# Projection of a four-layer kernel: in every tile the eight input runs first and the eight gate runs after them, with the statistics of the tile's own batches among its gates, and a second skip buffer

## The chip, the cores and the metric

One NeuronCore of a Trainium2 chip runs the whole program. The metric is the device time of one execution in microseconds (us); lower is better. Three runs of the kernel before gave 4415.28, 4422.65 and 4423.95 us, with the median at 4422.65 us.

## What is computed

Four layers are applied with a residual sum each: a gated state-space layer (0), two attention layers (1 and 2), and again a gated state-space layer (3). There are 32 batches of 128 tokens, 512 wide. The change touches only the first phase, the projection, of layers 0 and 3. Of the reference it computes this:

```python
xr, gate = jnp.split(x @ W_in.T, 2, axis=-1)          # 512 -> 2 x 1024
xr = xr + t_emb[:, None, :]
xc = conv(xr, W_conv, 4 taps, causal, per channel) + b_conv
xc = jax.nn.silu(xc)
mu, var = xc.mean(-1), xc.var(-1)
xn = (xc - mu) / jnp.sqrt(var + 1e-05) * ln_g + ln_b
Bm, Cm, dt = jnp.split(xn @ W_xproj.T, 3, axis=-1)    # 1024 -> 48
y = scan(...) + D * xn
return y * jax.nn.silu(gate) @ W_out.T
```

The projection phase leaves in memory the normalised `xn` (as a high and a low part), the skip term `D * xn`, and `silu(gate)`; it keeps the 48 projected columns and the mean and variance of every token on the chip. The recurrence phase reads them.

## The kernel before

The phase works on tiles of four batches (512 tokens), eight tiles T = 0 to 7, with a queue written out by hand for each engine; semaphores are the only order between engines.

PE (TensorE). `project_x(T, it)` multiplies 128 of the 1024 input channels by the tile: an input run of 12 matmuls (three partial products over four slices) into one of the two banks `pxr`. `project_gate(T, c)` is a gate run, also of 12 matmuls: one batch, 512 of the gate channels. `turn(n)` transposes the convolved batch n into the one two-bank buffer `ptr` (8 transposes); it waits on `z`, until DVE has read batch n-1 out of it. `xproj` multiplies the tile by the 48-column weight, `xproj_turn` transposes its result. Layer 3 reads its input in rows, so `turn_x(T + 1, b)` transposes the next tile's input, batch by batch (4 transposes each), through the one bank `pp`; its wait on `low` is the count of batches that DVE has read out of that bank. Layer 0 gets its input already transposed and has no `turn_x`.

DVE (VectorE). `evacuate(T, it)` adds the embedding and empties the `pxr` bank; `add_taps` adds three convolution taps on `pacc`; `split_low` takes the low part of the next tile's input (in layer 3 out of the bank `pp`); `centre(n)` is the statistics of batch n out of `ptr`, ending with the subtraction of the mean into `xn` (signal `z`), for which the `xn` buffer of batch n-2 must be free on POOL and ACT. ACT (ScalarE) does the first tap, the silu of convolution and gates, the high part of inputs (`split_high`), `rescale` by the standard deviation and `halves` (high part of `xn` and its squares). POOL (GpSimd) does for each batch in order: `shift` (adds ln_b), `skip_term` (D times xn, into `dx`), the next batch's `factor` (the inverse root) and `low_half`. SP stores the batch: `store_batch` waits for both halves, issues four stores of `xo`, waits for the skip term and stores `dx`.

There is one `dx` buffer, so `skip_term(n)` waits until the store of the skip term of batch n-1 has landed. In tile 0 the eight input runs come first and then the gates; in tiles 1 to 6 input and gate runs alternate, with the statistics of the tile before between them; in tile 7 the input runs come first, with statistics of tile 6 between, then the gates with those of tile 7.

## Time and profile before

| | us |
|---|---|
| profiled execution, its own time | 4415.49 |
| its span | 4413.70 |
| median of three runs | 4422.65 |
| layer 0, projection, from its first matmul to the start of the next phase | 11.15 to 581.75 |
| layer 3, the same | 3025.78 to 3601.52 |
| tile 1 to tile 7, starts of the first run, layer 0 | 76.53 to 434.33 |
| the same, layer 3 | 3097.89 to 3452.88 |

The page puts PE at 88% busy over the span, DVE at 67%, POOL at 41% and ACT at 30%. The other phases are the same instructions in both kernels. The two projections take about 1147 us of the 4414, so what happens elsewhere can be left out, and times below are those within one projection.

### The profile page before, as it was taken

How to read it: one execution, taken by the hardware profiler on the slowest of the kernel's cores; microseconds unless marked ns; L12 is line 12 of the kernel's file. 1: busy time of each engine (PE TensorE's matmuls, PEld its weight loads, DVE VectorE, ACT ScalarE, POOL GpSimd, SP SyncE). 2: the span in 40 equal slices, each digit the busy share in tenths (PEclk: the TensorE clock that was granted, in tenths of full speed). 3: DMA queues.
4: the chain of work that ended last, by engine and by line, in shares of the span. 5: the costliest groups of instructions: out<-in, count | busy, mean ns of one | idle time of the engine just before them, and what ended most of it. 6: DMA issues, size and time to landing. Idle time of an engine off the chain costs nothing. (4 is left out here: it accounts for less than half of the span.)

```text
span 4413.7 us, 67605 instructions
## 1 busy us (share of the span) xinstructions
PE 3882.5 (88%) x23976; PEld 2362.8 (54%) x23976; DVE 2944.5 (67%) x3022; ACT 1316.5 (30%) x1951; POOL 1811.0 (41%) x1456
## 2 busy tenths in 40 slices
PE   8999639999997599999849999997999818999999
PEld 6776413343332477777626777775777512443334
DVE  4666458999994555655445566653566537999996
ACT  3554301111113233333233333332455411111111
POOL 2555435555552123332312333323345534555555
PEclk9999859999998799999979999998999967999999
DMA  3565545666652122221221222213466545556653
GB/s 112 222 237 221 205 144 182 187 188 188 180 181 94 52 64 74 73 72 61 71 90 46 73 73 72 70 51 126 153 245 220 208 168 171 184 186 190 187 180 114
DMA packets 270306, 619.81 MB, mean 140 GB/s; under 512 B 34144, under 2 KB 36704, under 8 KB 270080
## 3 DMA queue, kind: packets, MB, share of 16 engines
q1 hardware_dynamic: 270080, 616.75, 42.3%
q8 instruction: 148, 2.42, 0.2%
q14 instruction: 78, 0.64, 0.0%
HBM read 380.46 MB, written 236.19 MB: 140 GB/s over the span
## 5 line engine op out<-in xcount | busy, mean ns | idle before, releaser
L1123 DVE CUSTOM_DVE_ANT_0 l3r_g<-l3r_g,l3r_pv,l3r_cf 128x1024 f32<-128x1024 f32 x512 | 674.3, 1339 | 77.9 <-PE l3r_pv L985 52.6
L1123 DVE CUSTOM_DVE_ANT_0 l0r_g<-l0r_g,l0r_pv,l0r_cf 128x1024 f32<-128x1024 f32 x512 | 674.1, 1339 | 74.8 <-PE l0r_pv L985 50.3
L985 PE MATMUL l3r_pv<-l3r_x,l3r_wv 32*128 32x512 f32 x1024 | 261.7, 510 | 26.0 <-POOL l3r_wv L910 19.9
L997 PE MATMUL l3r_py<-l3r_g,l3r_cd 128*32 128x512 f32 x2048 | 282.5, 625 | 2.1 <-POOL l3r_cd L923 2.1
L985 PE MATMUL l0r_pv<-l0r_x,l0r_wv 32*128 32x512 f32 x1024 | 260.9, 509 | 25.6 <-POOL l0r_wv L910 20.2
L997 PE MATMUL l0r_py<-l0r_g,l0r_cd 128*32 128x512 f32 x2048 | 281.2, 622 | 1.6 <-POOL l0r_cd L923 1.6
L985 PEld LDWEIGHTS l3r_pv<-l3r_x,l3r_wv 32*128 32x128 f32 x1024 | 97.2, 187 | 328.2 <-issue 227.1
L985 PEld LDWEIGHTS l0r_pv<-l0r_x,l0r_wv 32*128 32x128 f32 x1024 | 97.1, 187 | 326.2 <-issue 223.6
L1723 DVE RECIPROCAL l1h_rec<-l1h_ps_o 128x256 f32<-128x256 f32 x64 | 112.3, 1754 | 120.0 <-PE l1h_ps_o L1526 119.9
L1723 DVE RECIPROCAL l2h_rec<-l2h_ps_o 128x256 f32<-128x256 f32 x64 | 112.3, 1754 | 120.0 <-PE l2h_ps_o L1526 119.8
L558 DVE SCALAR_TENSOR_TENSOR l3a_pacc<-l3a_pad,l3a_wconv,l3a_pacc 128x512 f32<-128x512 f32 x192 | 144.8, 754 | 35.8 <-ACT l3a_pacc L433 31.2
L558 DVE SCALAR_TENSOR_TENSOR l0a_pacc<-l0a_pad,l0a_wconv,l0a_pacc 128x512 f32<-128x512 f32 x192 | 144.8, 754 | 34.5 <-ACT l0a_pacc L433 29.9
L670 POOL TENSOR_TENSOR l3a_dx<-l3a_xn,l3a_drow 128x1024 f32<-128x1024 f32 x32 | 76.3, 2384 | 215.2 <-DMA dx_s<-l3a_dx 215.1
L101 PE MATMUL l1h_ps_p<-l1h_xh,l1c_wh 128*128 128x512 f32 x384 | 161.3, 420 | 3.4 <-DVE l1h_xl L1715 2.9
L101 PE MATMUL l2h_ps_p<-l2h_xh,l2c_wh 128*128 128x512 f32 x384 | 160.9, 419 | 3.4 <-DVE l2h_xl L1715 2.9
L670 POOL TENSOR_TENSOR l0a_dx<-l0a_xn,l0a_drow 128x1024 f32<-128x1024 f32 x32 | 76.3, 2384 | 211.2 <-DMA dx_s<-l0a_dx 211.2
L103 PE MATMUL l2h_ps_p<-l2h_xl,l2c_wh 128*128 128x512 f32 x384 | 152.3, 397 | 0.0
L103 PE MATMUL l1h_ps_p<-l1h_xl,l1c_wh 128*128 128x512 f32 x384 | 152.0, 396 | 0.0
L102 PE MATMUL l2h_ps_p<-l2h_xh,l2c_wl 128*128 128x512 f32 x384 | 151.4, 394 | 0.0
L102 PE MATMUL l1h_ps_p<-l1h_xh,l1c_wl 128*128 128x512 f32 x384 | 150.9, 393 | 0.0
L1781 POOL TENSOR_TENSOR l1h_st<-l1h_veps,l1h_mhalf 128x1 f32<-128x1 f32 x32 | 17.6, 551 | 323.2 <-DVE l1h_veps L1689 323.2
L1781 POOL TENSOR_TENSOR l2h_st<-l2h_veps,l2h_mhalf 128x1 f32<-128x1 f32 x32 | 17.6, 551 | 322.9 <-DVE l2h_veps L1689 322.9
(404 smaller groups left out, 9862.7 us busy)
## 6 DMA issues: line engine op xcount, KB each, us to landing
xhl_s<-l0a_xo SPq DMA_DIRECT2D x128, 512.0 KB, 4.6
l0r_x<-xhl_s SPq DMA_DIRECT2D x128, 512.0 KB, 12.0
xhl_s<-l3a_xo SPq DMA_DIRECT2D x128, 512.0 KB, 4.6
l3r_x<-xhl_s SPq DMA_DIRECT2D x128, 512.0 KB, 11.8
gate_s<-l0a_gate SPq DMA_DIRECT2D x64, 256.0 KB, 3.3
dx_s<-l0a_dx SPq DMA_DIRECT2D x32, 512.0 KB, 5.0
l0r_crow<-feed_s SPq DMA_DIRECT2D x64, 256.0 KB
l0r_dx<-dx_s SPq DMA_DIRECT2D x32, 512.0 KB, 13.7
```

The source lines that it names most:

```text
L101: pe.matmul(out, wh, xh, start=first, stop=False)
L102: pe.matmul(out, wl, xh, start=False, stop=False)
L103: return pe.matmul(out, wh, xl, start=False, stop=last)
L558: dve.scalar_tensor_tensor(out=a, in0=pad[:, it % 2, :, c:c + S], scalar=wconv[:, it, c:c + 1], in1=a, op0=ALU.mult, op1=ALU.add).then_inc ...
L670: pool.tensor_tensor(dx[:, :], xn[:, r, :], drow[:, :], ALU.mult).then_inc(dxm, 1)
L985: last = pe.matmul(pv[j % 2][:, h * HALF:(h + 1) * HALF], wv[r, q, 2 * t + j % 2, :], x[r, q, t, j % 2, :], start=True, stop=True)
L997: last = pe.matmul(py[j * JW:(j + 1) * JW, h * HALF:(h + 1) * HALF], cd[:, q, t, j, :], g[:, t, j, h * HALF:(h + 1) * HALF], start=t == 0, ...
L1123: dve._custom_dve(bass.dve_ops.TENSOR_ADD_SAT, out=g[:, t, j, :], in0=g[:, (t - 1) % TS, j, :], in1=pv[j % 2][:, :], s0=cf[:, q, t, 0, j:j ...
L1723: dve.reciprocal(rec[:, :], ps_o[:, 2 * S:4 * S]).then_inc(rec_ok, 1)
L1781: pool.tensor_tensor(st[:, r, 2:3], veps[:, r:r + 1], mhalf[:, :], ALU.pow).then_inc(rs_ok, 1)
```

## The change

In every tile the eight input runs come first and the eight gate runs after them. The statistics of the tile's own four batches (`turn`, `xproj`, `xproj_turn`, `centre`) stand among these gates, and no longer among the runs of the following tile. The gates alternate between the banks `pg` and `pxr[1]` in all tiles (before: in the first and last). DVE evacuates run it+1 before it adds the taps of run it, in all tiles. The next tile's input is transposed after the input runs 4 to 7 (layer 3). The dt weight is folded after run 2 of tile 0, before: after run 4. The skip term gets a second buffer, the `stage` buffer that held weights, so that it waits for the store of batch n-2. In SP's queue the load of tile T + 1 stands at the start of tile T, behind the stores of the first two batches of tile T - 1 and ahead of those of its last two (the load of tile 1: among the weights of tile 0).

```diff
+        xo_st, dx_st = ph.sems("xo_st", 2), ph.sems("dx_st", 2)
         block = ph.block()
...
+        skip = (dx[:, :], stage[:, :, :].rearrange("p a n -> p (a n)"))
...
                 sp.wait_ge(dxm, n + 1)
-                sp.dma_start(dx_v[n // GB, n % GB, :, :, :], dx[:, :]).then_inc(dx_st, 16)
+                sp.dma_start(dx_v[n // GB, n % GB, :, :, :], skip[r]).then_inc(dx_st[r], 16)
...
-                    if it == 0:
-                        load(T + 1)
-                    store_gate(T, it)
-                    if it % 2 == 0 and TB * (T - 1) + it // 2 >= 2:
-                        store_batch(TB * (T - 1) + it // 2 - 2)
...
+                if c == 6:
+                    load(1)
+            for T in range(NT):
+                if 0 < T < NT - 1:
+                    load(T + 1)
+                if T:
+                    store_batch(TB * T - 2)
+                    store_batch(TB * T - 1)
+                for c in range(KI):
+                    store_gate(T, c)
+                    if c == 5:
+                        store_batch(TB * T)
+                    if c == 7:
+                        store_batch(TB * T + 1)
             store_batch(B - 2)
             store_batch(B - 1)
             for r in range(2):
                 sp.wait_ge(g_st[r], 16 * NT * KI // 2)
                 sp.wait_ge(xo_st[r], 64 * B // 2)
-            sp.wait_ge(dx_st, 16 * B)
+                sp.wait_ge(dx_st[r], 16 * B // 2)
...
-                if n == KI + 1:
-                    pe.wait_ge(g_ev, KI)
+                if it == 1:
+                    at_least(pe, g_ev, KI * T)
...
-                if in_a_row(T):
-                    at_least(pe, g_ev, n - 1)
-                    pe.wait_ge(xr_ev, KI * (T + 1))
-                else:
-                    at_least(pe, g_ev, n)
+                at_least(pe, g_ev, n - 1)
+                pe.wait_ge(xr_ev, KI * (T + 1))
...
                 pe.wait_ge(scaled, 3)
+                if rows:
+                    pe.wait_ge(low, 2 * TB)
...
                 if T:
                     pe.wait_ge(low, TB * T + b)
-                    pe.wait_ge(kept, 3)
                     at_least(pe, proj_ev, T - 1)
+                    if T == 1:
+                        pe.wait_ge(copied, 1)
...
-            for T in range(1, NT - 1):
+            for T in range(NT):
                 for it in range(KI):
                     project_x(T, it)
-                    if rows and it == KI - 1:
-                        turn_x(T + 1, TB - 1)
-                    project_gate(T, it)
-                    if it % 2 == 0:
-                        turn(TB * (T - 1) + it // 2)
-                    if it == 1:
-                        xproj(T - 1)
-                    if it == 3:
-                        xproj_turn(T - 1)
-                    if rows and TB <= it < KI - 1:
+                    if T == 0 and it == 2:
+                        fold_dt()
+                    if rows and it >= TB and T + 1 < NT:
                         turn_x(T + 1, it - TB)
...
+                for c in range(KI):
+                    project_gate(T, c)
+                    if T == 0 and c == 0:
+                        sum_weights()
+                    if c % 2 == 1:
+                        turn(TB * T + c // 2)
+                    if c == 2:
+                        xproj(T)
+                    if c == 4:
+                        xproj_turn(T)
...
+            for T in range(NT):
+                n = TB * T
                 for it in range(KI):
                     first_tap(T, it)
-                    if it == KI - 1:
-                        split_high(T + 1, TB - 1)
...
                     if it:
                         silu_conv(T, it - 1)
-                    elif T > 1:
-                        silu_conv(T - 1, KI - 1)
-                    n = TB * (T - 1) + it // 2
-                    silu_gate(T, it)
-                    if it == 2:
-                        copy_raw(T - 1)
-                    if TB <= it < KI - 1:
+                    if T:
+                        if it == 0:
+                            halves(n - 2)
+                        if it == 1:
+                            rescale(n - 1)
+                        if it == 2:
+                            halves(n - 1)
+                    if rows and it >= TB and T + 1 < NT:
                         split_high(T + 1, it - TB)
...
+                for c in range(KI):
+                    silu_gate(T, c)
+                    if c == 0:
+                        silu_conv(T, KI - 1)
+                    if c == 3:
+                        copy_raw(T)
+                    if not rows and c % 2 == 0 and T + 1 < NT:
+                        split_high(T + 1, c // 2)
+                    if c % 2 == 1 and c > 1 and T < NT - 1:
+                        rescale(n + c // 2 - 1)
+                    if c in (4, 6) and T < NT - 1:
+                        halves(n + c // 2 - 2)
+                    if c % 2 == 1 and c > 1 and T == NT - 1:
+                        halves(n + c // 2 - 1)
             halves(B - 1)
 
...
+            for T in range(NT):
+                evacuate(T, 0)
                 for it in range(KI):
-                    n = TB * (T - 1) + it // 2
-                    evacuate(T, it)
-                    if it % 2 == 1:
+                    if it + 1 < KI:
+                        evacuate(T, it + 1)
+                    add_taps(T, it)
+                    if T == 0 and it == 3:
+                        fold_gain()
+                    if rows and it >= TB and T + 1 < NT:
+                        split_low(T + 1, it - TB)
+                if T == 0:
+                    keep_sums()
+                for c in range(KI):
+                    n = TB * T + c // 2
+                    if not rows and c % 2 == 0 and T + 1 < NT:
+                        split_low(T + 1, c // 2)
+                    if c % 2 == 1:
                         centre(n)
-                    if it == 4:
-                        keep_projection(T - 1)
-                    if it == KI - 1:
-                        split_low(T + 1, TB - 1)
-                    add_taps(T, it)
-                    if TB <= it < KI - 1:
-                        split_low(T + 1, it - TB)
-            for it in range(KI):
-                n = TB * (NT - 2) + it // 2
-                evacuate(NT - 1, it)
-                if it % 2 == 1:
-                    centre(n)
-                if it == 4:
-                    keep_projection(NT - 2)
-                add_taps(NT - 1, it)
-            for b in range(TB):
-                centre(B - TB + b)
-                rescale_shift(B - TB + b)
-                if b == 2:
-                    keep_projection(NT - 1)
+                        if T == NT - 1:
+                            rescale_shift(n)
+                    if c == 5:
+                        keep_projection(T)
 
         @block.gpsimd
...
-                pool.tensor_tensor(dx[:, :], xn[:, r, :], drow[:, :], ALU.mult).then_inc(dxm, 1)
+                at_least(pool, dx_st[r], 16 * (n // 2))
+                pool.tensor_tensor(skip[r], xn[:, r, :], drow[:, :], ALU.mult).then_inc(dxm, 1)
```

Two places carry the prediction. The first is DVE's queue in layer 3, tile 2, behind the input runs 4 to 6. In both kernels L533 and L484 are `split_low`, L547 and L498 `evacuate`, L558 and L509 the taps, and L566 to L577 `centre`. The names behind "waits" are those of the semaphores' first owner, in layer 0. Before:

```order
L533 TENSOR_TENSOR l3a_xl<-l3a_pp,l3a_xh 128x4x128 [waits l0a_high]
L547 TENSOR_TENSOR l3a_pad<-l3a_pxr,l3a_temb 128x4x128 [waits l0a_tap0,l0a_taps,l0a_xr_mm]
L566 BN_STATS l3a_bst<-l3a_ptr 128x6 [waits l0a_bn,l0a_tr_mm]
L567 BN_STATS l3a_bst<-l3a_ptr 128x6
L570 BN_AGGR l3s_stat<-l3a_bst 128x2 [waits l0a_bn]
L573 TENSOR_SCALAR l3a_veps<-l3s_stat 128x1 [waits l0a_rstd,l0a_bn]
L577 SCALAR_TENSOR_TENSOR l3a_xn<-l3a_ptr,l3s_stat,l3a_grow 128x1024 [waits l0a_dxm,l0a_xol,l0a_ss]
L558 SCALAR_TENSOR_TENSOR l3a_pacc<-l3a_pad,l3a_wconv,l3a_pacc 128x512 [waits l0a_xr_ev,l0a_tap0]
L558 SCALAR_TENSOR_TENSOR l3a_pacc<-l3a_pad,l3a_wconv,l3a_pacc 128x512 [waits l0a_taps] x2
L533 TENSOR_TENSOR l3a_xl<-l3a_pp,l3a_xh 128x4x128 [waits l0a_high]
```

and now:

```order
L498 TENSOR_TENSOR l3a_pad<-l3a_pxr,l3a_temb 128x4x128 [waits l0a_tap0,l0a_taps,l0a_xr_mm]
L509 SCALAR_TENSOR_TENSOR l3a_pacc<-l3a_pad,l3a_wconv,l3a_pacc 128x512 [waits l0a_xr_ev,l0a_tap0]
L509 SCALAR_TENSOR_TENSOR l3a_pacc<-l3a_pad,l3a_wconv,l3a_pacc 128x512 [waits l0a_taps] x2
L484 TENSOR_TENSOR l3a_xl<-l3a_pp,l3a_xh 128x4x128 [waits l0a_high]
L498 TENSOR_TENSOR l3a_pad<-l3a_pxr,l3a_temb 128x4x128 [waits l0a_tap0,l0a_taps,l0a_xr_mm]
L509 SCALAR_TENSOR_TENSOR l3a_pacc<-l3a_pad,l3a_wconv,l3a_pacc 128x512 [waits l0a_xr_ev,l0a_tap0]
L509 SCALAR_TENSOR_TENSOR l3a_pacc<-l3a_pad,l3a_wconv,l3a_pacc 128x512 [waits l0a_taps] x2
L484 TENSOR_TENSOR l3a_xl<-l3a_pp,l3a_xh 128x4x128 [waits l0a_high]
L498 TENSOR_TENSOR l3a_pad<-l3a_pxr,l3a_temb 128x4x128 [waits l0a_tap0,l0a_taps,l0a_xr_mm]
```

The statistics have left this place; the reading of the `pp` bank (L484) now stands behind the taps of the same run, ahead of the evacuation of the run that PE is to do next. The second place is PE's queue beside it: `turn_x` (L354 before, L350 now), input runs (first row of each), gate runs, and `turn` (L363). Before:

```order
L354 MATMUL l3a_pp<-l3a_ident,l3a_xt 128x128 [waits l0a_kept,l0a_proj_ev,l0a_low,l0a_x_loaded]
L354 MATMUL l3a_pp<-l3a_ident,l3a_xt 128x128 x3
L101 MATMUL l3a_pxr<-l3a_xh,l3a_wih 128x512 [waits l0a_xr_ev]
...
L101 MATMUL l3a_pg<-l3a_wih,l3a_xh 128x512 [waits l0a_g_ev]
...
L363 MATMUL l3a_ptr<-l3a_ident,l3a_xc 128x128 [waits l0a_z]
L363 MATMUL l3a_ptr<-l3a_ident,l3a_xc 128x128 x7
L354 MATMUL l3a_pp<-l3a_ident,l3a_xt 128x128 [waits l0a_kept,l0a_proj_ev,l0a_low,l0a_x_loaded]
L354 MATMUL l3a_pp<-l3a_ident,l3a_xt 128x128 x3
```

and now:

```order
L350 MATMUL l3a_pp<-l3a_ident,l3a_xt 128x128 [waits l0a_proj_ev,l0a_low,l0a_x_loaded]
L350 MATMUL l3a_pp<-l3a_ident,l3a_xt 128x128 x3
L101 MATMUL l3a_pxr<-l3a_xh,l3a_wih 128x512 [waits l0a_xr_ev]
...
L350 MATMUL l3a_pp<-l3a_ident,l3a_xt 128x128 [waits l0a_proj_ev,l0a_low,l0a_x_loaded]
L350 MATMUL l3a_pp<-l3a_ident,l3a_xt 128x128 x3
L101 MATMUL l3a_pxr<-l3a_xh,l3a_wih 128x512 [waits l0a_xr_ev]
```

Between two groups of `turn_x` there stood an input run, a gate run and every second time a `turn`; now there stands one input run.

## Rows read from the trace of the kernel before

**Rows 1.** PE's timeline, first input runs of tiles 1 and 7, both layers (start, us)

```profile
76.53 0.50 PE L101 MATMUL l0a_pxr<-l0a_xh,l0a_wih 128*128 128x512 f32 x1 [1.93 <-DVE l0a_xl L536]
...
434.33 0.50 PE L101 MATMUL l0a_pxr<-l0a_xh,l0a_wih 128*128 128x512 f32 x1 [2.62 <-DVE l0a_xl L536]
...
3097.89 0.50 PE L101 MATMUL l3a_pxr<-l3a_xh,l3a_wih 128*128 128x512 f32 x1 [1.46 <-DVE l3a_xl L533]
...
3452.88 0.50 PE L101 MATMUL l3a_pxr<-l3a_xh,l3a_wih 128*128 128x512 f32 x1 [1.08 <-DVE l3a_xl L533]
```

**Rows 2.** DVE's timeline, first instruction of the phase behind each projection

```profile
581.79 1.76 DVE L747 TENSOR_TENSOR l0b_mean_w<-l0s_stat,l0s_wsum 128x1536 f32<-128x1536 f32 x1 [22.05 <-PEq L43]
...
3601.56 1.76 DVE L747 TENSOR_TENSOR l3b_mean_w<-l3s_stat,l3s_wsum 128x1536 f32<-128x1536 f32 x1 [22.06 <-PEq L43]
```

**Rows 3.** POOL's timeline in layer 0, one skip term

```profile
440.15 2.37 POOL L670 TENSOR_TENSOR l0a_dx<-l0a_xn,l0a_drow 128x1024 f32<-128x1024 f32 x1 [6.43 <-DMA dx_s<-l0a_dx]
...
443.01 2.38 POOL L675 TENSOR_TENSOR l0a_xo<-l0a_xn,l0a_xo 128x1024 fp32r<-128x1024 f32 x1
```

**Rows 4.** SP's queue in layer 0: the stores of one batch

```profile
431.48 3.44 SPq L238 DMA_DIRECT2D xhl_s<-l0a_xo  x4
434.97 1.33 SPq L241 DMA_DIRECT2D dx_s<-l0a_dx  x1
```

**Rows 5.** Waits of layer 0, 116 to 470 us (engine, line, releaser: us, times, longest)

```profile
POOL l0a_dx L670 <- DMA dx_s<-l0a_dx: 155.1, 24, 8.3
...
PE l0a_pxr L101 <- DVE l0a_xl L536: 15.1, 6, 3.5
```

**Rows 6.** PE's timeline in layer 3, tile 2: input transposes, then two runs

```profile
3195.55 0.60 PE L354 MATMUL l3a_pp<-l3a_ident,l3a_xt 128*128 128x128 f32 x4
3195.91 0.48 PE L101 MATMUL l3a_pxr<-l3a_xh,l3a_wih 128*128 128x512 f32 x1
...
3198.79 0.39 PE L101 MATMUL l3a_pg<-l3a_wih,l3a_xh 128*128 128x512 f32 x1
```

**Rows 7.** DVE's timeline in layer 3, tile 2

```profile
3198.99 0.69 DVE L547 TENSOR_TENSOR l3a_pad<-l3a_pxr,l3a_temb 128x512 f32<-128x512 f32 x1 [1.42 <-PE l3a_pxr L103]
3199.60 0.69 DVE L566 BATCH_NORM_STATS2 l3a_bst<-l3a_ptr 128x6 f32<-128x512 f32 x1
...
3202.54 2.33 DVE L558 SCALAR_TENSOR_TENSOR l3a_pacc<-l3a_pad,l3a_wconv,l3a_pacc 128x512 f32<-128x512 f32 x3
3204.78 0.68 DVE L533 TENSOR_TENSOR l3a_xl<-l3a_pp,l3a_xh 128x512 fp32r<-128x512 f32 x1
```

**Rows 8.** DMA issues of layer 3's tiles: queue, count, KB each, median us to landing

```profile
l3a_xt<-x_s SPq DMA_DIRECT2D x24, 256.0 KB, 4.0
```

**Rows 9.** PE's timeline, an input run behind a wait, of tiles 4 and 5

```profile
253.14 0.50 PE L101 MATMUL l0a_pxr<-l0a_xh,l0a_wih 128*128 128x512 f32 x1 [2.15 <-DVE l0a_xl L536]
...
256.04 0.39 PE L101 MATMUL l0a_pg<-l0a_wih,l0a_xh 128*128 128x512 f32 x1
...
312.45 0.50 PE L101 MATMUL l0a_pxr<-l0a_xh,l0a_wih 128*128 128x512 f32 x1 [2.99 <-DVE l0a_xl L536]
...
316.90 0.40 PE L101 MATMUL l0a_pg<-l0a_wih,l0a_xh 128*128 128x512 f32 x1
```

**Rows 10.** PE's timeline, tile 0 of layer 3: fold and first gate

```profile
3050.63 1.95 PE L316 MATMUL l3a_pp<-l3a_wdt,l3a_dx 16*128 16x16 f32 x16 [1.67 <-DMA l3a_drow<-L_D]
...
3066.87 0.47 PE L101 MATMUL l3a_pg<-l3a_wih,l3a_xh 128*128 128x512 f32 x1 [4.16 <-DVE l3a_pad L547]
```

**Rows 11.** DVE's timeline, tile 7 of layer 3: statistics and shift

```profile
3551.65 0.69 DVE L566 BATCH_NORM_STATS2 l3a_bst<-l3a_ptr 128x6 f32<-128x512 f32 x1
...
3553.39 1.29 DVE L577 SCALAR_TENSOR_TENSOR l3a_xn<-l3a_ptr,l3s_stat,l3a_grow 128x1024 f32<-128x1024 f32 x1
3562.35 3.28 DVE L584 SCALAR_TENSOR_TENSOR l3a_xn<-l3a_xn,l3s_stat,l3a_brow 128x1024 f32<-128x1024 f32 x1 [7.67 <-POOL l3s_stat L659]
```

**Rows 12.** POOL's timeline, last low half of layer 0

```profile
569.66 2.34 POOL L675 TENSOR_TENSOR l0a_xo<-l0a_xn,l0a_xo 128x1024 fp32r<-128x1024 f32 x1
```

More of the change, by code:

```diff
@@ L196, in gate_part, with gate_bank @@
             return (c % TB, c // TB) if T == 0 else (c // 2, c % 2)
-        def in_a_row(T):
-            return T in (0, NT - 1)
-        def gate_bank(T, c):
-            return pxr[1] if in_a_row(T) and c % 2 else pg
+        def gate_bank(c):
+            return pxr[1] if c % 2 else pg
         def turned(T, b):
@@ L258, in _ @@
                     sp.dma_start(dst, src).then_inc(loaded, 16)
-            for T in range(NT - 1):
-                for it in range(KI):
-                    if it == 0:
-                        load(T + 1)
-                    store_gate(T, it)
-                    if it % 2 == 0 and TB * (T - 1) + it // 2 >= 2:
-                        store_batch(TB * (T - 1) + it // 2 - 2)
-            for n in range(B - TB - 6, B - TB - 1):
-                store_batch(n)
-            for c in range(KI):
-                store_gate(NT - 1, c)
-                if c == 2:
-                    store_batch(B - TB - 1)
-                if c % 2 == 1 and c > 3:
-                    store_batch(B - TB + c // 2 - 2)
+                if c == 6:
[12 more added lines that the diff above has]
+                        store_batch(TB * T + 1)
             store_batch(B - 2)
@@ L331, in xproj @@
                 if rows:
-                    pe.wait_ge(low, TB * (T + 2) if T + 2 <= NT else TB * NT)
+                    pe.wait_ge(low, TB * min(T + 2, NT))
                 for k in range(KI):
@@ L439, in silu_gate @@
                 at_least(act, g_st[c % 2], 16 * (n // 2))
-                act.activation(gate[:, c % 2, :], gate_bank(T, c)[:, :], ACT.Silu).then_inc(g_ev, 1)
+                act.activation(gate[:, c % 2, :], gate_bank(c)[:, :], ACT.Silu).then_inc(g_ev, 1)
             def silu_conv(T, it):
@@ L486, in _ @@
                 for it in range(KI):
                     first_tap(T, it)
-                    if it == KI - 1:
-                        split_high(T + 1, TB - 1)
+                    if T == 0:
+                        for c in (2 * it + 2, 2 * it + 3):
+                            if c < NW:
+                                high_weight(c)
                     if it:
                         silu_conv(T, it - 1)
-                    elif T > 1:
-                        silu_conv(T - 1, KI - 1)
@@ L494, in _ @@
-                    n = TB * (T - 1) + it // 2
-                    silu_gate(T, it)
-                    if it == 2:
-                        copy_raw(T - 1)
-                    if TB <= it < KI - 1:
-                        split_high(T + 1, it - TB)
-                    if it % 2 == 0 and n >= 1:
-                        rescale(n - 1)
-                    if it % 2 == 1 and n >= 1:
-                        halves(n - 1)
-            T = NT - 1
-            for it in range(KI):
-                first_tap(T, it)
-                silu_conv(T - 1 if it == 0 else T, (it - 1) % KI)
-                n = TB * (T - 1) + it // 2
-                if it == 2:
-                    copy_raw(T - 1)
-                if it % 2 == 0:
-                    rescale(n - 1)
-                if it % 2 == 1:
-                    halves(n - 1)
@@ L515, in _ @@
-            silu_conv(T, KI - 1)
-            for c in range(KI):
-                silu_gate(T, c)
-                if c == 0:
-                    rescale(B - TB - 1)
-                if c == 1:
-                    halves(B - TB - 1)
-                if c == 3:
-                    copy_raw(T)
-                if c % 2 == 1 and c > 1:
-                    halves(B - TB + c // 2 - 1)
+                    if T:
[5 more added lines that the diff above has]
+                            halves(n - 1)
```

60 lines of the change are left out of this document (2 added, 58 removed).

## The prediction

> **What bounds the kernel now.** The change touches only the two projections, so I read these alone. First the timeline of PE, at the first input run of tiles 1 and 7 [rows 1]. Six tiles take 434.33 - 76.53 = 357.8 us in layer 0, 59.63 each, and 3452.88 - 3097.89 = 355.0 us in layer 3, 59.17 each. The reader is to see how little PE waits: ahead of these tiles 1.1 us in layer 3 and, by the list of waits, 15.1 us in six tiles of layer 0 [rows 1, 5]. So PE's own work is 58.1 us a tile in layer 3 and, when I take off 2.5 us of wait and 0.8 us for runs at the lower clock, 56.3 in layer 0. Tiles 1 to 6 are bound by PE. POOL waits 155.1 us there for the one skip buffer [rows 5]; that is cover, and costs nothing while PE is busy.
>
> It is otherwise at the end. From tile 7's first run to the next phase 581.79 - 434.33 = 147.5 us pass in layer 0 and 148.7 in layer 3 [rows 1, 2], for a tile whose work on PE is under 60. There the statistics of eight batches queue for the one `dx` buffer: after the skip term POOL's low half ends at 445.4, the four stores and that of `dx` take 4.8 us to issue, and the next skip term waits 6.4 us or more for the landing [rows 3, 4].
>
> **The tail: what is gained.** Now tile 7 holds only its own four batches, and POOL needs 2.4 + 0.5 + 2.4 = 5.3 us a batch with the shift on DVE [rows 3], under the 6.8 us that PE works from one `turn` to the next (two gate runs of 2.8, `turn` 0.8, `xproj_turn` 0.4, estimated from a gate run's length being that of an input run, [rows 6]). The last `turn` ends with PE, at about 60.2 us (below). Behind it: statistics 3.4 with the wait for PE (3553.39 + 1.29 - 3551.65 = 3.0 without it, [rows 11]), shift 3.3, skip term 2.4, low half 2.4 [rows 3, 11], together 11.5; then stores and the change of phase as now, 581.79 - 572.0 = 9.8 [rows 2, 12]. Sum 81.5 us. The gain is 66.0 us in layer 0 and 67.2 in layer 3.
>
> **Tile 0: what is lost.** The work of its statistics moves here: 58.1 - 16 runs of 2.85 - four `turn_x` of 0.36 = 11 us [rows 6]. The fold waits for the last small load (1.7 us now, [rows 10]), which is tied to the weights and not to PE; placed two runs earlier it waits some 7 us. Before, the gates began 3066.87 - 3050.63 = 16.2 us behind it. Now five runs follow it: fold 1.9 [rows 10], a run at the lower clock 4.5, and then DVE's five evacuations and four sets of taps (3.0 + 9.0) and its fold: 20 us, so 4 more. In layer 3 the three turns of the chain described next stand in it too: about 39 us, so 23 more. With the wait ahead of tile 1 gone (1.9 and 1.5) and layer 3's `turn_x` moved (1.4), tile 1 starts 13 us later in layer 0 and 31 in layer 3.
>
> **Layer 0, tiles 1 to 6.** PE does eight runs in 22.9 us. DVE has 3199.60 - 3198.99 = 0.6 us for an evacuation, start to start, and 2.24 for the taps [rows 7], and begins late: the first evacuation stands behind the statistics of the fourth batch, whose `xn` buffer POOL frees about 4.0 us into the next tile. (POOL's chain for the first two batches, 15.4 us, begins when ACT has passed gate 3, 11.4 us ahead of the tile's end.) With 1.3 us for the subtraction the last evacuation ends at 5.3 + 8 x 0.6 + 7 x 2.24 = 25.8, and PE has waited 2.9 us ahead of its gates. In the gates ACT, POOL and SP have slack by the same count. Tile: 56.3 + 2.9 + half of the clock's 1.55 (below) = 60.0, against 59.63: six tiles 2 us more. Bounds 58.4 (none of the clock's price, runs in a row switching less) and 61.5.
>
> **Layer 3, tiles 1 to 6: the chain.** The bank `pp` is single. `turn_x` of batch b waits until DVE has read batch b - 1, and DVE does that behind the taps of the run before; PE's next input run stands behind `turn_x`, and DVE's next evacuation waits for that run. So from one reading of the bank to the next, nothing overlaps: reading 0.68, `turn_x` 0.36, input run until its evacuation starts 3198.99 - 3195.91 = 3.08, evacuation 0.69, taps 2.24 [rows 6, 7], sum 7.05 us, of which PE works 0.36 + 2.88 = 3.24 and is idle 3.8. It happens three times a tile (batches 1 to 3). Before, a gate run and statistics filled that time. To it comes about 1.1 us at the start of the tile (POOL's lateness as above; the load is issued behind the stores of a batch, 4.8 us, itself in four parts, and lands 4.0 later, at about 15 us, when run 5 is due; taken at its low end because runs in a row switch less) [rows 4, 8].
>
> And the clock: behind a wait of 2.15 us an input run took 256.04 - 253.14 = 2.90 us, behind one of 2.99 us 316.90 - 312.45 = 4.45, with the granted clock at its lower level for most of it [rows 9]. I take 1.55 us for each of the four runs behind a wait of 2.9 us or more. Tile: 58.1 + 1.1 + 3 x 3.8 + 4 x 1.55 = 76.8. Bounds: 70.6 if the clock never falls, 81 if each such run is slow from end to end. Six tiles: 6 x (76.8 - 59.17) = 106 us more.
>
> The Trainium skill (Perfetto Trace Analysis, Optimization Strategy) advises to interleave stretches in which different engines are the most contended. By it the alternating order was the better one, and the separated input runs, where DVE has more to do than PE, pay for that.
>
> **Sum.** Layer 0: 13 + 2 - 66 = -51. Layer 3: 31 + 106 - 67 = +70. Together +19: 4415.5 + 19 = 4434 us, made against the profiled execution's own time. That time lies at the low end of the runs; their median is 7 us higher. A difference of 0.2% (9 us) is about what a measurement of this kernel can tell from none.
>
> **Rivals.**
> (1) The clock stays up. Idle times of 3.8 us between runs of 3.2 leave it at its higher level. For it: after 2.15 us it stayed up [rows 9]; against it: 2.99 us was enough. Then layer 3 has 6 x 11.4 = 68, tile 0 about 25, so +26, and layer 0 is at 58.4 a tile, -63: together -36, 4379, faster. It decides at a price of about 1.0 us a run (1.55 x 36 / 55), where the sum is zero. The Trainium skill (TensorE: Matmul & The Clock Gate, The HAM clock gate) says that the array's clock is halved after idle time and released by activity; rows 9 agree that a wait brings it down. Chance 0.15, and 0.12 for something between it and the forecast, near 4410.
> (2) Slow throughout layer 3's input runs: 81 us a tile, 4460. For it: PE is idle more than half of the chain. Chance 0.13.
> (3) The chain is not there: PE's `turn_x` waits for nothing, and layer 3 is as layer 0. Then both gain 51 us, 4314. Against it stands the count on `low` in the code and in the order of both queues; only a reading of mine that is wrong would bring it. 0.03.
> (4) The second buffer does nothing: the tail is held by the stores themselves, five of them in 4.8 us of issue for each batch [rows 4]. POOL's chain of 5.3 us is only just longer. Then some 10 us of each tail stay: 4454. 0.05.
>
> **How the numbers follow.** The forecast has 0.52, with 4415 to 4460 of its own, mostly from the 70.6 to 81 of layer 3's tile. The range leaves out the far ends of (1), (2) and (3): 4388 to 4462. Slower by over 0.2%: the forecast's greater part, (2) and (4), 0.62. Faster: (1), (3) and part of what lies between, 0.20. Within: 0.18.
>
> **What would show it.** Right: in layer 3's tiles three waits of PE of 3.5 to 4 us each, for DVE's `xl` out of `pp`, and tiles of 75 to 79 us; granted clock clearly under 1.0 in these stretches; layer 0's tiles at 59 to 61; POOL's wait for the store of the skip term nearly gone; both tails near 81 us. Wrong: tiles of layer 3 under 72 (clock), or PE waiting in the gates for ACT or DVE, which I count as nothing: ACT's `rescale` stands ahead of the next gate's silu, and if POOL's inverse root comes late, two gates are held.

## The result and the profile after

The changed kernel takes 4514.1 us (median of 4 runs, 4511.7 to 4518.5), the kernel before, run beside it, 4419.5 us. The ratio is 1.0215, with a 95% interval of 1.0197 to 1.0233: 2.2% slower. The forecast was 4434 us, slower; the time lies 52 us above the end of its range. The profiled execution has a span of 4512.4 us against 4413.7, so 98.7 us are to be accounted for.

Timelines of PE and DVE in the changed kernel: the first input runs of tiles 1 and 7, and the first instruction behind each projection, as in [rows 1, 2].

```profile
91.17 0.48 PE L101 MATMUL l0a_pxr<-l0a_xh,l0a_wih 128*128 128x512 f32 x1
...
477.06 0.50 PE L101 MATMUL l0a_pxr<-l0a_xh,l0a_wih 128*128 128x512 f32 x1
...
564.98 1.76 DVE L684 TENSOR_TENSOR l0b_mean_w<-l0s_stat,l0s_wsum 128x1536 f32<-128x1536 f32 x1 [16.48 <-PEq L43]
...
3024.73 0.47 PE L101 MATMUL l3a_pxr<-l3a_xh,l3a_wih 128*128 128x512 f32 x1 [2.71 <-POOL l3a_wil L590]
...
3124.57 0.48 PE L101 MATMUL l3a_pxr<-l3a_xh,l3a_wih 128*128 128x512 f32 x1
...
3613.70 0.48 PE L101 MATMUL l3a_pxr<-l3a_xh,l3a_wih 128*128 128x512 f32 x1
...
3702.80 1.76 DVE L684 TENSOR_TENSOR l3b_mean_w<-l3s_stat,l3s_wsum 128x1536 f32<-128x1536 f32 x1 [16.56 <-PEq L43]
```

The same first input run of layer 3 in the kernel before, which the rows ahead did not show:

```profile
3032.16 0.47 PE L101 MATMUL l3a_pxr<-l3a_xh,l3a_wih 128*128 128x512 f32 x1 [2.71 <-POOL l3a_wil L653]
```

Six tiles are (477.06 - 91.17) / 6 = 64.3 us each in layer 0 and (3613.70 - 3124.57) / 6 = 81.5 in layer 3; the tails, from tile 7 to the next phase, are 87.9 and 89.1. Against [rows 1, 2]:

| stage | predicted, us | measured, us |
|---|---|---|
| layer 0, tile 0 (80.5 against 65.4) | +13 | +15.1 |
| layer 0, tiles 1 to 6 | +2 | +28.1 |
| layer 0, tail | -66 | -59.5 |
| layer 3, tile 0 (99.8 against 65.7) | +31 | +34.1 |
| layer 3, tiles 1 to 6 | +106 | +134.1 |
| layer 3, tail | -67 | -59.6 |
| everything else | 0 | +6.4 |
| sum | +19 | +98.7 |

The signs are right in all six rows of the projections, and the two rows of tiles 1 to 6 hold 54 us of the 80 missed.

Stretches of tiles 1 to 6, kernel before, layer 3 and layer 0 (window, length, busy us and instructions of each engine, granted clock, DMA share, GB/s):

```profile
core 0: us, PE busy (x) PEld busy (x) DVE busy (x) ACT busy (x) POOL busy (x), PEclk, DMA share, GB/s
3097.00:3453.00 356.00, 348.60 (x1561) 258.26 (x1562) 222.23 (x341) 176.37 (x264) 171.08 (x90) 1.00 0.57 210
76.00:434.00 358.00, 342.65 (x1464) 251.63 (x1464) 236.52 (x340) 174.87 (x263) 175.48 (x90) 0.99 0.56 209
```

and the changed kernel:

```profile
3124.00:3614.00 490.00, 395.93 (x1569) 287.91 (x1568) 223.43 (x343) 183.19 (x271) 183.56 (x97) 0.90 0.45 168
91.00:477.00 386.00, 353.30 (x1467) 256.31 (x1466) 233.32 (x342) 180.25 (x270) 187.08 (x97) 0.96 0.58 212
```

Nearly the same number of matmuls keeps PE busy 47 us longer in layer 3: that is the clock, down from 1.00 to 0.90 on the mean, 7.9 us a tile (e6 below tests it). The rest of the 22.3 us a tile is idle: 94 us in six tiles against 7.

The chain in layer 3 is there as forecast. PE's timeline, tile 3 (the four `turn_x`, and the first matmul behind the first of them):

```profile
3306.28 1.12 PE L350 MATMUL l3a_pp<-l3a_ident,l3a_xt 128*128 128x128 f32 x4 [3.86 <-DMA l3a_xt<-x_s]
3307.04 0.78 PE L101 MATMUL l3a_pxr<-l3a_xh,l3a_wih 128*128 128x512 f32 x1
...
3315.92 1.09 PE L350 MATMUL l3a_pp<-l3a_ident,l3a_xt 128*128 128x128 f32 x4 [3.67 <-issue]
...
3324.27 0.63 PE L350 MATMUL l3a_pp<-l3a_ident,l3a_xt 128*128 128x128 f32 x4 [3.67 <-issue]
...
3332.92 1.09 PE L350 MATMUL l3a_pp<-l3a_ident,l3a_xt 128*128 128x128 f32 x4 [3.67 <-issue]
```

Three idles of 3.67 us. The profile puts them down to "issue"; what ends them is seen on DVE, whose reading of the bank (L484) starts at 3315.14, 0.8 us ahead of the next `turn_x`. The periods are 9.64, 8.35 and 8.65 us where the parts make 7.05.

What the prediction did not have is in layer 0. POOL, SP's queue, ACT and PE, at the gates of tile 2:

```profile
172.97 2.41 POOL L607 TENSOR_TENSOR l0a_stage<-l0a_xn,l0a_drow 128x1024 f32<-128x1024 f32 x1 [0.51 <-DMA dx_s<-l0a_stage]
194.79 0.55 POOL L596 TENSOR_TENSOR l0s_stat<-l0a_veps,l0a_mhalf 128x1 f32<-128x1 f32 x1 [19.41 <-DVE l0a_veps L524]
195.31 2.35 POOL L612 TENSOR_TENSOR l0a_xo<-l0a_xn,l0a_xo 128x1024 fp32r<-128x1024 f32 x1
...
197.73 3.42 SPq L235 DMA_DIRECT2D xhl_s<-l0a_xo  x4
...
208.89 0.60 ACT L412 ACTIVATE l0a_gate<-l0a_pg 128x512 f32<-128x512 f32 x1 [16.25 <-DMA gate_s<-l0a_gate]
...
209.54 0.79 PE L101 MATMUL l0a_pg<-l0a_wih,l0a_xh 128*128 128x512 f32 x1 [2.99 <-ACT l0a_gate L412]
```

On POOL the next batch's `factor` (L596) stands ahead of `low_half` (L612). At a tile's last batch the next batch belongs to the next tile, whose statistics now come in its gates, so `factor` waits 19.4 us for them, and `low_half`, which needs nothing of them, waits with it. SP stores that batch only at 197.73, and all gate stores of the tile stand behind it in SP's queue. The third gate finds both gate buffers full, ACT waits 16.3 us, and PE 3.0.

### The profile page after: what moved, and what is told of

The parts are those of the page before. It is cut to its first block and busy times, and to the rows that moved or that the text cites. A ratio compares the mean times of both kernels' runs of the same rounds, so it can differ in the third digit from the quotient of the medians.

```text
span 4512.4 us, 67690 instructions
## 1 busy us (share of the span) xinstructions
PE 3934.2 (87%) x23976; PEld 2394.8 (53%) x23976; DVE 2937.0 (65%) x3022; ACT 1319.8 (29%) x1951; POOL 1814.2 (40%) x1456
## 5 line engine op out<-in xcount | busy, mean ns | idle before, releaser
L509 DVE SCALAR_TENSOR_TENSOR l0a_pacc<-l0a_pad,l0a_wconv,l0a_pacc 128x512 f32<-128x512 f32 x192 | 144.1, 754 | 16.2 <-ACT l0a_pacc L405 11.5
L509 DVE SCALAR_TENSOR_TENSOR l3a_pacc<-l3a_pad,l3a_wconv,l3a_pacc 128x512 f32<-128x512 f32 x192 | 144.6, 753 | 13.2 <-ACT l3a_pacc L405 8.7
L1532 ACT ACTIVATE l1h_pt<-l1h_ps_t 128x512 f32<-128x512 f32 x128 | 75.7, 592 | 247.5 <-PE l1h_ps_t L1449 247.5
L1532 ACT ACTIVATE l2h_pt<-l2h_ps_t 128x512 f32<-128x512 f32 x128 | 75.7, 591 | 241.8 <-PE l2h_ps_t L1449 241.8
```

The costliest lines, as they stand in the source:

```text
L509: dve.scalar_tensor_tensor(out=a, in0=pad[:, it % 2, :, c:c + S], scalar=wconv[:, it, c:c + 1], in1=a, op0=ALU.mult, op1=ALU.add).then_inc ...
L1532: act.activation(pt[:, u % 2, :, :], ps_t[:, :].rearrange("p (h s) -> p h s", h=HG), ACT.Copy).then_inc(pt_ok, 1)
```

## The experiments

The kernel before ran beside each group at 4415 to 4420 us. Its two stages of interest stand in the first row.

| kernel | us | layer 0: tile / tail | layer 3: tile / tail |
|---|---|---|---|
| before | 4415 to 4420 | 59.6 / 147.5 | 59.2 / 148.7 |
| changed | 4514.1 | 64.3 / 87.9 | 81.5 / 89.1 |
| e1 low half first | 4482.4 | 62.0 / 87.2 | 79.0 / 87.8 |
| e2 early reading | 4441.5 | 64.0 / 88.0 | 71.8 / 89.6 |
| e3 before, two buffers | 4330.1 | 59.9 / 106.4 | 59.2 / 105.6 |
| e9 the kernel of e3 again | 4332.4 | 59.9 / 104.6 | 59.2 / 103.3 |
| e4 changed, one buffer | 4719.5 | 76.2 / 119.6 | 92.6 / 120.0 |
| e5 four edits | 4408.9 | 62.0 / 87.4 | 68.2 / 87.4 |
| e6 filled idle | 4487.5 | 64.3 / 88.0 | 76.0 / 91.4 |
| e10 e5, earlier high part | 4377.7 | 62.0 / 88.7 | 64.9 / 87.3 |

**e1.** POOL's order, one edit:

```diff
+                if n % TB == TB - 1:
+                    low_half(n)
                 if n + 1 < B:
                     factor(n + 1)
-                low_half(n)
+                if n % TB < TB - 1:
+                    low_half(n)
```

> The changed kernel with one edit on POOL: for the last batch of each tile the low half is written ahead of the next batch's factor, not behind it. Theory A (the factor of the next tile's first batch waits some 20 us for statistics in the gates; the low half behind it, and so SP's stores of that batch and all gate stores behind them, are that late, and ACT and PE wait for a gate buffer): layer 0's tiles fall from 64.3 us to about 60.4, layer 3's lose about 1 us, ACT's wait for the gate stores is nearly gone, each tail loses some 5 us; the kernel takes about 4469 us (4460 to 4480) where the changed kernel takes 4514. Rival B (two gate buffers and the stores' own pace hold ACT, whatever the order on POOL): no change, 4514, and ACT's wait stays.

32 us less: theory A, 2 us above its range. In both layers ACT's wait for the gate stores (89.5 us in six tiles of layer 0) and PE's wait for ACT are gone from the list of waits; what is left of PE's in layer 0 is 0.49 us ahead of the third input run and the wait ahead of the first gate, and that one is as long as in the changed kernel. The list, tiles 1 to 6 of layer 0 (releaser: us, times, longest):

```profile
PE l0a_pg L101 <- DVE l0a_pad L498: 18.5, 6, 3.1
```

The tile is 1.6 us longer than expected: the first gate's run behind that wait takes 4.58 us (242.53 to 247.11, the granted clock at its lower level for most of it), where 3.0 is a run at the higher level. In layer 3 the tile fell by 2.5 us where 1 was expected. The tails, which were to lose some 5 us each, lost about 1 (87.2 and 87.8).

**e2.** Layer 3 only: the high part on ACT, before behind `silu_conv`, and the low part on DVE, before behind `add_taps`:

```diff
                     first_tap(T, it)
...
+                    if rows and it >= TB and T + 1 < NT:
+                        split_high(T + 1, it - TB)
                     if it:
                         silu_conv(T, it - 1)
...
+                    if rows and TB - 1 <= it < KI - 1 and T + 1 < NT:
+                        split_low(T + 1, it + 1 - TB)
                     add_taps(T, it)
```

> The changed kernel with layer 3's reading of the transposed input moved: on DVE it stands ahead of the taps of the run before, on ACT directly behind the first tap and ahead of the silu; the fold of the gain one run earlier. Layer 0 is not touched. Theory A (the chain over the single bank, of which the taps and the evacuation are the idle part): the three idles of 3.67 us a tile go, and with them the lower clock; layer 3's tile falls from 81.5 us to 64 or 65, its tile 0 by 17; together some 117 us less: about 4397 us (4385 to 4410). Rival B (DVE's own work in the input runs, or the late load, holds PE anyway, and the idle only moves): the gain stays under 40 us.

Between the two theories: 73 us less, where A had 117 and B under 40. PE's timeline, tile 2:

```profile
3201.70 0.66 PE L350 MATMUL l3a_pp<-l3a_ident,l3a_xt 128*128 128x128 f32 x4 [2.99 <-DMA l3a_xt<-x_s]
...
3206.55 0.60 PE L350 MATMUL l3a_pp<-l3a_ident,l3a_xt 128*128 128x128 f32 x4
...
3209.79 0.60 PE L350 MATMUL l3a_pp<-l3a_ident,l3a_xt 128*128 128x128 f32 x4
...
3214.69 0.63 PE L350 MATMUL l3a_pp<-l3a_ident,l3a_xt 128*128 128x128 f32 x4 [1.50 <-issue]
3217.77 0.76 PE L101 MATMUL l3a_pg<-l3a_wih,l3a_xh 128*128 128x512 f32 x1 [2.45 <-DVE l3a_pad L498]
```

Two of the three idles are gone and the third is 1.5 us. In their place stands DVE's lateness ahead of the first gate, 2.45 us, which the idles had covered, and the wait for the load stays. So the chain was real, but taking it away gives back only what the next wait does not take.

**e3 and e4.** The second buffer alone, and the new order alone:

```diff
-                at_least(pool, dx_st, 16 * n)
-                pool.tensor_tensor(dx[:, :], xn[:, r, :], drow[:, :], ALU.mult).then_inc(dxm, 1)
+                at_least(pool, dx_st[r], 16 * (n // 2))
+                pool.tensor_tensor(skip[r], xn[:, r, :], drow[:, :], ALU.mult).then_inc(dxm, 1)
```

> The kernel before with the second skip buffer alone; the order of all queues stays. Theory A (the tail is POOL waiting for the one buffer; tiles 1 to 6 are bound by PE and its wait there is cover): tiles 1 to 6 stay at 59.6 and 59.2 us, each tail falls from 147 us to about 96 (PE's runs of tile 7 and a backlog of one or two batches), together about 4320 us (4310 to 4345). Rival B (the stores themselves set the pace of the tail): each tail loses 20 us at most, 4380 or more.

4330.1 us, ratio 0.9805 (0.9788 to 0.9821): theory A, with tiles as before and tails at 106.4 and 105.6, which is 10 us longer than A had them. This kernel beats both. Its starts in layer 0:

```profile
76.83 0.50 PE L101 MATMUL l0a_pxr<-l0a_xh,l0a_wih 128*128 128x512 f32 x1 [1.93 <-DVE l0a_xl L537]
...
435.94 0.50 PE L101 MATMUL l0a_pxr<-l0a_xh,l0a_wih 128*128 128x512 f32 x1 [2.72 <-DVE l0a_xl L537]
...
542.38 1.76 DVE L748 TENSOR_TENSOR l0b_mean_w<-l0s_stat,l0s_wsum 128x1536 f32<-128x1536 f32 x1 [15.89 <-PEq L43]
```

> The changed kernel with one skip buffer, as the kernel before had. Theory A (the tail's gain of some 60 us each came from the second buffer): POOL takes some 14 us a batch and each tile of 4 batches 56 us of it, the tails grow by 15 to 25 us, and late buffers in the next tile add to the tiles in between: 4545 to 4620 us. Rival B (the tail's gain came from the order alone, since tile 7 holds only its own four batches): within 15 us of the changed kernel, 4514.

4719.5 us: A in sign, but 100 us above its range. The tails grew by 31 us where 15 to 25 were said; the tiles between grew by 11.8 and 11.1 us each, which I had priced at almost nothing. The list of waits, tiles 1 to 6 of layer 0:

```profile
POOL l0a_dx L606 <- DMA dx_s<-l0a_dx: 123.2, 18, 8.7
ACT l0a_gate L411 <- DMA gate_s<-l0a_gate: 89.7, 6, 16.3
DVE l0a_xl L486 <- ACT l0a_xh L392: 86.0, 14, 14.1
ACT l0a_xn L429 <- POOL l0s_stat L595: 85.6, 17, 8.0
...
PE l0a_pxr L101 <- DVE l0a_pad L497: 68.9, 18, 7.5
```

POOL's wait for the skip buffer, about as long in the kernel before [rows 5], was covered there; here ACT waits for POOL's factor behind it (85.6 us), the first taps stand behind ACT, and PE in the end waits 68.9 us for DVE to empty its banks, 11.5 us a tile (4.3 us in all six tiles of the changed kernel). With one buffer the new order costs 4719.5 - 4415.4 = 304 us, with two 4514.1 - 4330.1 = 184. The second buffer is worth 85 us in the old order and 205 in the new one.

**e5 and e10.** The waits of the new order that a change of place can take out: the edits of e1 and e2, and

```diff
-                if 0 < T < NT - 1:
+                if not rows and 0 < T < NT - 1:
                     load(T + 1)
...
                     store_gate(T, c)
+                    if rows and c == 1 and T < NT - 2:
+                        load(T + 2)
```

with layer 0's fold back at its old run.

> The changed kernel with four edits together: the low half ahead of the factor (as e1), the early reading of layer 3's transposed input (as e2), layer 3's load of tile T + 2 issued behind the second gate of tile T, and layer 0's fold at its old place. From e1 and e2: layer 0 takes 539 us (e1) less 4 for the fold, 535; layer 3 takes 611 us (e2), less 2.5 a tile for the gates and their buffers and less 3.0 of load wait with 1.5 of lower clock a tile, some 565 to 580. Theory A (with every wait that the new order made by accident gone, what is left is DVE's backlog ahead of the gates, some 3 us a tile with its slow run, in both layers, so the separated order stays the slower one): 4370 us (4350 to 4385), faster than the kernel before through the tails, but slower than the old order with two skip buffers (4330). Rival B (the separated order was only badly queued and is as good as the old one): 4330 or less.

4408.9 us, ratio 0.9978 (0.9967 to 0.9990). Neither theory: the time is 39 us above A's 4370 and outside its range. The load wait is gone, but layer 3's tile is 68.2 us where e2's 71.8 less the load wait, the lower clock behind it and the gates would be near 65. Timeline of DVE, tile 3 of layer 3:

```profile
3249.42 0.69 DVE L500 TENSOR_TENSOR l3a_pad<-l3a_pxr,l3a_temb 128x512 f32<-128x512 f32 x1
3251.49 0.69 DVE L486 TENSOR_TENSOR l3a_xl<-l3a_pp,l3a_xh 128x512 fp32r<-128x512 f32 x1 [1.37 <-ACT l3a_xh L391]
3252.09 2.33 DVE L511 SCALAR_TENSOR_TENSOR l3a_pacc<-l3a_pad,l3a_wconv,l3a_pacc 128x512 f32<-128x512 f32 x3
3254.51 0.69 DVE L500 TENSOR_TENSOR l3a_pad<-l3a_pxr,l3a_temb 128x512 f32<-128x512 f32 x1
```

A loop of 5.09 us, of DVE and ACT: evacuation, ACT's first tap and high part (1.37 us idle), reading, taps. I had moved the reading ahead of the taps but left it behind ACT's tap, which waits for the evacuation. e10 moves that one (shown against e5):

```diff
+                    if rows and it >= TB and T + 1 < NT:
+                        split_high(T + 1, it - TB)
                     first_tap(T, it)
...
-                    if rows and it >= TB and T + 1 < NT:
-                        split_high(T + 1, it - TB)
```

> e5 with one edit on ACT: in layer 3 the high part of the transposed input is read out of the bank ahead of the first tap of the same run, not behind it. In e5 (4409 us, layer 3's tiles 68.2) DVE's reading still waits 1.37 us three times a tile: evacuation 0.6, wait for ACT's first tap and high part, reading 0.6, taps 2.3, a period of 5.09 us where PE needs 3.3. Theory A (that loop through ACT is what is left of the chain): the period falls to DVE's own 0.6 + 0.6 + 2.24 = 3.5 us, layer 3's tile to 63 us (62 to 65.5, with the 3 us ahead of the gates and their slow run left), the kernel to about 4375 us (4370 to 4390). Rival B (DVE is late by its whole work anyway, and the wait comes back ahead of the first gate): the tile stays above 67 us, the kernel within 10 us of e5.

4377.7 us, ratio 0.9903: theory A in the times. The loop fell to 3243.03 - 3238.94 = 4.09 us and not to DVE's own 3.5, since DVE still waits 0.37 us for ACT. Its timeline, tile 3 of layer 3:

```profile
3238.94 2.33 DVE L511 SCALAR_TENSOR_TENSOR l3a_pacc<-l3a_pad,l3a_wconv,l3a_pacc 128x512 f32<-128x512 f32 x3
...
3242.43 0.69 DVE L486 TENSOR_TENSOR l3a_xl<-l3a_pp,l3a_xh 128x512 fp32r<-128x512 f32 x1 [0.37 <-ACT l3a_xh L391]
3243.03 2.33 DVE L511 SCALAR_TENSOR_TENSOR l3a_pacc<-l3a_pad,l3a_wconv,l3a_pacc 128x512 f32<-128x512 f32 x3
```

The tile is 64.9 us, and what is left of PE's waits in the input runs is 13.3 us in six tiles, beside 14.7 ahead of the first gate:

```profile
PE l3a_pg L101 <- DVE l3a_pad L500: 14.7, 6, 2.4
PE l3a_pp L352 <- issue: 13.3, 18, 1.3
```

Even so the separated order stays at 62.0 and 64.9 us a tile against 59.9 and 59.2 in e3. Its tile 0 is 11 and 19 us longer as well, its tails are 16 to 18 us shorter, and in all it is 48 us behind.

**e6.** The clock by itself, in the changed kernel's chain:

```diff
+                if T > 1 and b:
+                    at_least(pe, z, TB * (T - 1))
+                    for _ in range(10):
+                        pe.matmul(ptr[:, 0:TW], wih[:, 0, 0, :], xh[:, (T - 1) % 2, 0, :], start=True, stop=True)
+                if T:
+                    pe.wait_ge(low, TB * T + b)
```

> The changed kernel with more work on PE: in tiles 1 to 6 of layer 3, ahead of the input transposes of batches 1 to 3 and before they wait, ten matmuls of 128 x 512 into a bank that nobody reads, some 2.5 us of the 3.67 us idle. Nothing else is changed. Theory A (each idle of 3.67 us costs a lower clock in the run behind it: the periods between the transposes are 9.65, 8.03 and 9.0 us where the parts at the full clock add up to 7.05): the 180 added matmuls take the place of the idle, the clock stays up, the periods fall to about 7.1 us and the kernel by 25 to 35 us: about 4484. Rival B (the periods are long for another reason, in DVE or ACT, and the clock is no part of it): no change or, since the added work can spill over the idle, up to 20 us slower.

27 us less, with 180 matmuls more: theory A. PE's timeline, tile 3 (L351 the added matmuls, L355 `turn_x`):

```profile
3299.73 2.50 PE L351 MATMUL l3a_ptr<-l3a_xh,l3a_wih 128*128 128x512 f32 x10
3303.52 0.66 PE L355 MATMUL l3a_pp<-l3a_ident,l3a_xt 128*128 128x128 f32 x4 [1.29 <-DVE l3a_xl L489]
...
3306.81 2.50 PE L351 MATMUL l3a_ptr<-l3a_xh,l3a_wih 128*128 128x512 f32 x10
3310.60 0.66 PE L355 MATMUL l3a_pp<-l3a_ident,l3a_xt 128*128 128x128 f32 x4 [1.29 <-DVE l3a_xl L489]
...
3317.68 0.66 PE L355 MATMUL l3a_pp<-l3a_ident,l3a_xt 128*128 128x128 f32 x4 [1.30 <-DVE l3a_xl L489]
```

The periods are 7.08 us, the 7.05 of the prediction's parts; the granted clock of the stretch is 0.99. The tile falls by 5.5 us: the clock's price of the three runs is 1.8 us each.

**e7, e8, e11, e12.** What is left of e3's tail. Each is e3 with an edit of order. In e7 SP stores the skip term ahead of the parts of `xo`; in e8 the low half of batch 27 stands ahead of the factor; in e11 that of batch 28; e12 is e7 and e11 together.

```diff
             def store_batch(n):
                 r = n % 2
+                sp.wait_ge(dxm, n + 1)
+                sp.dma_start(dx_v[n // GB, n % GB, :, :, :], skip[r]).then_inc(dx_st[r], 16)
                 sp.wait_ge(xoh, n + 1)
...
-                sp.wait_ge(dxm, n + 1)
-                sp.dma_start(dx_v[n // GB, n % GB, :, :, :], skip[r]).then_inc(dx_st[r], 16)
```

> The kernel before with two skip buffers (e3, 4330 us) and one edit in SP's queue: the skip term of a batch is stored ahead of its four parts of xo, not behind them. In e3 the last skip terms of a tail still waited 5.96 and 2.56 us for the landing of a store, and ACT waited 3.24 and 5.58 us for the stores of xo. Theory A (what is left of the tail, 106 us, hangs on the skip term's store standing last): each tail loses 5 to 9 us, 4315. Rival B (ACT's wait for the stores of xo, which now start 1.3 us later, takes over): within 5 us of e3.

> The kernel before with two skip buffers (e3) and one edit on POOL: for batch 27, the last of tile 6, the low half is written ahead of the next batch's factor, which in e3 waited 3.95 us for the first statistics of tile 7 with the low half and SP's stores of that batch behind it. Theory A (in each tail of e3, 106 us, that lateness is handed on from POOL by SP's queue to the last batches): each tail loses 2 to 4 us, the kernel about 6 us against e3 run beside it. Rival B (the tail's end is paced by the four and one stores of each batch, 4.8 us of issue and the landing, whatever their start): within 2 us of e3, no difference that can be measured.

> The same kernel as e3, run again beside e8 to compare with: 4330 us, tiles 1 to 6 at 59.9 and 59.2 us, tails at 106.

> The kernel before with two skip buffers (e3) and the low half of batch 28 ahead of the next factor. The trace of e8 showed that its edit stood at the wrong batch: the factor that waits (3.97 us) is that of batch 29, and the low half behind it that of batch 28, the first of tile 7. Theory A (the lateness is handed on to the end of the tail by SP's queue): the stores of batch 28 are issued some 4 us earlier and each tail loses 2 to 4 us, 4325. Rival B (the gate stores ahead of and behind those stores and the pace of the last three batches set the end): within 3 us of e3, no difference that can be measured.

> e11 with the skip term stored ahead of the four parts of xo (e7's edit) as well. In e7 the wait of POOL for the skip buffer went and ACT's wait for the xo buffer took its place (4.33 and 5.58 us). Theory A (each hides the other, and both go only together): 4318 to 4325. Rival B (the pace of SP's stores, 4.8 us of issue a batch and the landing of four parts, is the end of the tail): within 3 us of e3, 4330.

4331.3, 4330.1, 4332.9 and 4332.2 us, and 4332.4 for e3 run again as e9: no difference in any. The tails of all six traces lie between 103.3 and 106.4 us, those of one kernel, e3 and e9, among them. e8 tells nothing, since its edit stood at a batch whose factor had not waited. In e7 and e12 POOL no longer waits for a store; it waits about 2.7 and 3.0 us for ACT's half instead. ACT waits 4.3 and 5.6 us for the stores of `xo` in e7, where it had 3.2 and 5.6 in e3, and from POOL's last low half to the next phase 10.5 to 11.2 us pass instead of 9.8. The reason that no order helps shows in the stretches. First e3, then the kernel before, each in the tail of layer 0:

```profile
520.00:530.00 10.00, 0.00 (x0) 0.00 (x0) 3.28 (x1) 3.16 (x6) 7.17 (x4) 0.50 1.03 388
530.00:540.00 10.00, 0.00 (x0) 0.00 (x0) 0.00 (x0) 0.00 (x0) 2.62 (x2) 0.50 1.02 383
```

```profile
550.00:560.00 10.00, 0.00 (x0) 0.00 (x0) 3.28 (x1) 0.23 (x1) 5.15 (x3) 0.50 0.30 115
560.00:570.00 10.00, 0.00 (x0) 0.00 (x0) 0.00 (x0) 1.87 (x3) 2.64 (x2) 0.50 0.69 260
```

With one buffer the 16 DMA engines had room; with two they are full at 383 to 388 GB/s until the phase ends (in e9 at 389 and, in the last stretch, 346), in the new order too (388 and 392 from 545 to 563 us). That the stores bound the tail's end is argued from this and from three kernels with changed orders whose time did not move (e7, e11, e12); storing fewer bytes was not tried.

## Why the prediction was wrong

**Layer 0, tiles 1 to 6 (+2, measured +28): the step that failed.** "In the gates ACT, POOL and SP have slack by the same count." That count gave each engine's work and not the order of its queue. It looked at `factor` as a wait of ACT, and not at what stands behind it on POOL. e1 shows the lost 2.3 us a tile to be this: a `factor` 19 us early in the queue, a low half behind it, a batch's stores behind that in SP's queue, gate stores behind those, and ACT's and PE's gates. The prediction had named a late inverse root ("if POOL's inverse root comes late, two gates are held"), as a wait of ACT alone, and given it nothing. The same edit takes 2.5 us a tile out of layer 3 and 32 us out of the kernel. The other 2.0 us a tile of layer 0 are sizes: waits of 3.08 and 0.49 us where 2.9 was taken, and 1.3 us more of PE's work, most of it the lower clock behind the first wait (e1, tile 3: 4.58 us), whose price of 1.5 us is paid in full where half was taken.

**Layer 3, tiles 1 to 6 (+106, measured +134).** The mechanism was right to a tenth of a microsecond: three waits, 3.67 us where 3.8 was said, and in e6 periods of 7.08 against 7.05. Mis-sized was the clock, 7.9 us a tile by PE's busy time against 6.2. The 6.2 were four runs at 1.55; the three of the chain cost 1.8 each by e6, the fourth can only be the one behind the load's wait, and three of the four `turn_x` shown above took 1.09 to 1.12 us where the fourth took 0.63, which the sum left out. Mis-sized was also the start with the load, 1.1 in the sum: the load's wait alone is 20.1 us in six tiles, 3.4 a tile. And PE waits 1.0 us at the fifth gate for ACT, which was taken as nothing; e1 removes it, so it is the failed step of layer 0 again. The bound of 81 us for the tile was too low by 0.5, because it had only 1.1 us for the load and nothing for the gate.

**The tails (-66 and -67, measured -60 twice).** The sum had no wait of the skip term for its store any more. Two are left in the new order, of 4.30 and 3.00 us for the last two batches in layer 0. In that layer's tail the last `turn` ends 62.6 us behind the start of tile 7, where 60.2 was said; from there to POOL's last low half 15.4 us pass, where 11.5 was said, and then 9.9, where 9.8 was. So the stretch that holds these waits has the larger part of what was missed. Rival (4) falls in its first half, that the second buffer does nothing: by e3 and e9 it gives 41 to 45 us of each tail with the old order. Its second half, stores that hold the end, fits what is left, 6 to 8 us a tail where it said 10, and is argued, not shown. The further 14 to 19 us are the new order's, in which tile 7 no longer carries tile 6's statistics. The split depends on which comes first: the order alone (e4) takes 28 us from each tail, and the buffer then 31.

**Tile 0 (+13 and +31, measured +15 and +34).** Right within 3 us. The fold waits 7.4 us in layer 3, where 7 was said.

**Rival (1), that the clock stays up,** falls: the granted clock of layer 3's stretch was 0.90. Its evidence was also read too simply: behind the wait of 1.93 us at tile 1 [rows 1] the run of the kernel before took 80.98 - 76.53 = 4.45 us, so waits shorter than the 2.15 us quoted could already bring the clock down. Rival (2), 4460 for a clock low throughout, was nearer than the forecast in time and not in cause: of the four runs of tile 3 none is at the lower level from end to end, and the rest of the miss is elsewhere. (3) falls with the waits.

**The rule on interleaving** (the Trainium skill, Perfetto Trace Analysis, Optimization Strategy) agrees with the runs: with the waits of e1, e2, e5 and e10 taken out, the separated order is still 2.1 and 5.7 us a tile behind e3. In layer 0 what is left is DVE's lateness ahead of the first gate (3.1 us) and the lower clock behind it. That no other order of separated runs would do as well as e3 is not shown.

## What to carry to other kernels

When a stage is moved in hand-written queues, don't only count each engine's work: for each instruction that will now wait longer, write down what stands behind it on its own queue, and who waits for that, until the list ends; here one 0.5 us operation at a tile's border cost 32 us. Price a change that holds two ideas as two: the buffer alone gained 2.0%, the order alone lost 6.9%. A chain over a single buffer is removed only when its reader waits for nothing of the next round on any engine (e2 and e10 each took one such wait away), and what it had hidden comes up then.
